# The weights of the second query convolution, made ready in the gate stage of an attention kernel

## The chip, the cores and the metric

The kernel runs on one core of a Trainium2 chip. The metric is the device time of one execution, in microseconds (us). An execution was also recorded by the hardware profiler. The engines are PE (TensorE, matrix multiplication), DVE (VectorE), ACT (ScalarE), POOL (GpSimd) and SP (SyncE, which here only issues DMAs). A line such as L1680 is a line of the kernel before.

## What is computed

Two layers, each an attention branch multiplied by a gated feed-forward branch and added to x. The edit concerns the first layer's second query convolution (`qc2_w`, 1024 x 1024 x 3 taps, causal, one group), and borders on the gate branch of the same layer:

```python
def _forward(x, w_qkv, w_o, qc1_w, qc1_b, qc2_w, qc2_b, kc1_w, ...):
    qkv = x @ w_qkv.T
    ...
    q = _causal_conv1d(_causal_conv1d(q, qc1_w, qc1_b, N_HEADS), qc2_w, qc2_b, 1)
    ...
    q = q.reshape(B, S, N_HEADS, HEAD_DIM) + 0.5 * k_mean[:, :, None, :]
    q = _rope(_l2norm(q.transpose(0, 2, 1, 3)), cos, sin)
    ...
def reference(...):                       # x is 2 x 1024 x 512
    xn = _layernorm(x)
    s = _L0_attn_ref(xn, ...)             # 16 query heads, 4 key heads of 64
    g = _silu(_L0_ffn_ref(xn, ...))       # relu(x up)^2 down, plus a routed part
    x = x + s * g
    ...                                   # second layer, untouched
```

## The kernel before

The program is a row of stages, one after another, that share on-chip buffers: the gate stage (names beginning a_, 13.5 to 320 us of the trace), the project stage (b_, q, k, v projections and the first convolutions, 320 to 589), the query stage (c_, the second query convolution, normalisation and rotation, 589 to 1051), attention (d_), then the second layer (e_, f_, h_). Each engine runs its own instruction list in program order, and semaphores are the only link between the lists. Nothing is scheduled at run time.

**Gate stage.** Four chunks of 512 tokens. For each, PE transposes the normalised tokens (`transposes`, L245), multiplies them with the latent and up weights (L273, 10 units of 12 matmuls, in chunk 0 in float32), then the logits and four output tiles (L300, L305). ACT copies the transposes out (`transposed`, L322 and L324), then one `relu` for each unit (L337), which must leave one of two PSUM banks before PE can fill it again. DVE squares each relu (L472), and after the units combines four output tiles. In the project stage `find_peaks` (L819) needs maxima that DVE takes over what ACT prepared at L890 to L892 from loaded weight rows.

**Query stage.** The three-tap convolution is done in a transformed form (six slices, fewer products than the taps would need). For each of 8 output tiles m of 128 channels, the float32 weight rows (128 x 3072) come in by DMA (L1256, L1476). DVE makes sums of taps (`sums`, L1673 and L1675), ACT scales and rounds a slice to fp16 (`highs`, L1457), DVE takes the rest to fp16 (`lows`, L1680). The scale needs the largest norm: ACT squares the rows (`ends_of`, L1469, L1472), PE adds them over partitions (`bound`, L1360), POOL takes a root, DVE inverts it (L1647 to L1656). PE then runs six slices of 24 matmuls (L1420). Around these stand DVE's `combine` (L1699 to L1727), which turns six slices into outputs, the squares and norms (L1498, L1330, L1336), the spreading of norms (L1353), DVE's `units` (L1750) and `remainder` (L1754), and POOL's rotation (L1599 to L1603). SP stores the finished parts (L1269, L1272) and loads the tables, the keys and `k_mean` (L1258) at the start.

## Time and profile before

| | |
|---|---|
| time, median of 3 (lowest to highest) | 2363.93 us (2362.97 to 2368.98) |
| profiled execution, its own time | 2369.5 us |
| its span | 2367.7 us |
| PE busy over the span | 2058.6 us, 87% |
| DVE, ACT, POOL busy | 1489.3, 1100.8, 771.9 us |
| gate stage | 13.5 to 320 us |
| project stage | 320 to 589 us |
| query stage | 589 to 1051 us |

Times in the trace are counted from the start of the span. "Busy" is the time with an instruction at work. In a timeline, what stands in brackets is how long the engine had been idle, and whose instruction released it. PEclk is the clock granted to PE, as a share of its full speed.

### The profile page before, as it was taken

The numbers are of one execution on the slowest core, as the hardware profiler recorded it, in microseconds if no ns is written. First come the engines' busy times: TensorE is split into PE (matmuls) and PEld (weight loads), VectorE is DVE, ScalarE is ACT, GpSimd is POOL, SyncE is SP. The second block draws the span as 40 slices with busy tenths as digits, with TensorE's granted clock in tenths as the row PEclk, the third lists the DMA queues.
The fourth block names the chain that finished last, engine by engine and source line by source line (L and its number), as shares of the span: only waits on it lengthen the run. The fifth ranks groups of instructions, "written<-read, shape, count | busy, mean of one in ns | idle before, by whom it ended". The sixth has DMA issues, their size and how long they took to land. (4 is left out here: it accounts for less than half of the span.)

```text
span 2367.7 us, 46673 instructions
## 1 busy us (share of the span) xinstructions
PE 2058.6 (87%) x19128; PEld 1009.8 (43%) x19128; DVE 1489.3 (63%) x2992; ACT 1100.8 (46%) x1987; POOL 771.9 (33%) x735
## 2 busy tenths in 40 slices
PE   7999989998647898979999789987588888888878
PEld 3444435555213333445555434443244444443434
DVE  3534354443559999716777725445888888888813
ACT  1212135555324333227777502324277777777760
POOL 0102212222447456504444402223343333433310
PEclk9999999999879899989999989997799999999999
DMA  6120101101412121362222264132936455364424
GB/s 240 36 89 36 67 19 32 32 14 44 140 43 83 54 67 32 107 208 75 90 82 76 76 175 143 58 79 76 216 59 84 69 72 81 58 89 65 59 79 142
DMA packets 149338, 198.03 MB, mean 84 GB/s; under 512 B 57154, under 2 KB 85956, under 8 KB 146564
## 3 DMA queue, kind: packets, MB, share of 16 engines
q1 hardware_dynamic: 147540, 181.41, 30.9%
q10 hardware_dynamic: 1584, 13.63, 1.6%
q8 instruction: 151, 2.47, 0.5%
q14 instruction: 63, 0.52, 0.1%
HBM read 134.69 MB, written 60.29 MB: 82 GB/s over the span
## 5 line engine op out<-in xcount | busy, mean ns | idle before, releaser
L3112 DVE TENSOR_REDUCE f_chunk_max<-f_ps_a 128x64 f32<-128x1024 f32 x320 | 319.7, 1033 | 47.4 <-PE f_ps_a L2856 25.0
L2985 ACT ACTIVATE conv_in<-f_ps_s 128x512 f32<-128x512 f32 x480 | 258.5, 602 | 86.6 <-PE f_ps_s L2887 42.7
L2856 PE MATMUL f_ps_a<-conv_in 128*32 128x512 bf16 (+3 forms) x3072 | 201.0, 340 | 42.1 <-DVE f_chunk_max L3112 25.4
L2078 ACT ACTIVATE d_probs<-d_ps_s,d_shift 128x512 f32<-128x512 f32 (+3 forms) x384 | 196.7, 584 | 82.7 <-PE d_ps_s L2017 72.8
L2887 PE MATMUL f_ps_s<-f_qs,f_ks 128*32 128x512 bf16 x2304 | 208.3, 382 | 23.3 <-ACT f_qs L2976 14.7
L1420 PE MATMUL c_ps_c<-conv_in,c_wT 128*128 128x512 f16 x768 | 186.2, 402 | 18.5 <-DVE c_odd L1721 14.1
L3052 POOL TENSOR_SCALAR f_absent<-f_rest 128x576 f32<-128x576 f32 x32 | 54.4, 1700 | 304.9 <-DVE f_rest L3129 180.7
L2909 PE MATMUL f_ps_o<-conv_in,f_v 128*32 128x512 f32 (+2 forms) x1152 | 125.9, 522 | 28.3 <-ACT conv_in L2985 27.4
L2976 ACT ACTIVATE f_qs<-f_ps_s 32x512 bf16<-32x512 f32 x192 | 112.8, 587 | 75.6 <-PE f_ps_s L2870 73.3
L2028 PE MATMUL d_ps_o<-d_probs,conv_in 128*64 128x512 f32 (+3 forms) x768 | 146.1, 488 | 0.0
L2856 PEld LDWEIGHTS f_ps_a<-conv_in 128*32 128x32 bf16 x3072 | 71.8, 98 | 164.3 <-DVE f_chunk_max L3112 68.6
L2388 PE MATMUL e_ps_s<-e_oT,conv_in 128*128 128x512 f32 x256 | 118.7, 626 | 23.2 <-DVEq L64 17.4
L2012 PE MATMUL d_ps_s<-conv_in 128*64 128x512 f16 (+3 forms) x768 | 126.4, 330 | 8.8 <-POOL d_ones L2086 8.8
L2145 DVE RECIPROCAL d_inverse<-d_ps_n 128x1024 f32<-128x1024 f32 x16 | 104.9, 6558 | 44.2 <-PE d_ps_n L2039 44.2
L1420 PEld LDWEIGHTS c_ps_c<-conv_in,c_wT 128*128 128x128 f16 x768 | 77.2, 103 | 129.9 <-issue 36.8
L2016 PE MATMUL d_ps_s<-conv_in 128*64 128x512 f16 (+3 forms) x384 | 124.8, 329 | 0.0
L2017 PE MATMUL d_ps_s<-conv_in 128*64 128x512 f16 (+3 forms) x384 | 124.7, 329 | 0.0
L300 PE MATMUL a_ps_d<-conv_in,conv_more 128*128 128x512 f32 x256 | 119.2, 621 | 0.0
L2887 PEld LDWEIGHTS f_ps_s<-f_qs,f_ks 128*32 128x32 bf16 x2304 | 59.6, 95 | 106.8 <-ACT conv_in L2985 35.0
L798 POOL TENSOR_TENSOR conv_in<-b_tiles,conv_in 128x1024 f16<-128x1024 f32 x16 | 34.1, 2131 | 186.6 <-ACT conv_more L958 186.6
L2388 PEld LDWEIGHTS e_ps_s<-e_oT,conv_in 128*128 128x128 f32 x256 | 51.0, 201 | 89.8 <-issue 82.4
L1420 PE MATMUL c_ps_c<-conv_more,c_wT 128*128 128x512 f16 x384 | 88.3, 384 | 0.0
(364 smaller groups left out, 4451.5 us busy)
## 6 DMA issues: line engine op xcount, KB each, us to landing
conv_in<-qk SPq DMA_DIRECT2D x96, 128.0 KB, 4.0
f_qs<-qk SPq DMA_DIRECT2D x96, 128.0 KB, 4.8
conv_in<-q_parts SPq DMA_DIRECT2D x8, 1024.0 KB, 5.1
o0T<-d_stage SPq DMA_DIRECT2D x16, 512.0 KB, 3.2
conv_in<-o0T SPq DMA_DIRECT2D x4, 2048.0 KB, 10.6
qk<-e_part SPq DMA_DIRECT2D x12, 640.0 KB, 4.9
f_qs<-qk SPq DMA_DIRECT2D x96, 64.0 KB, 4.7
rows<-in_qc_w ACTq DMA_DIRECT2D x3, 1536.0 KB, 7.0
```

What stands on the lines that cost most here:

```text
L1420: last = pe.matmul(ps_c[q % RING][:], wT[i][:, w, k, :], conv_of.of(t, x, k), start=(k == 0 and w == 0 and x == 0), stop=(k == MQ - 1 and ...
L2012: pe.matmul(out[sides[e], lo - low:], k_high[b][:, keys[e]], q[b][:, h, lo:hi], start=True, stop=False)
L2016: pe.matmul(out[sides[0], lo - low:], k_low[b][:, keys[0]], q[b][:, h, lo:hi], start=False, stop=True)
L2017: pe.matmul(out[sides[1], lo - low:], k_low[b][:, keys[1]], q[b][:, h, lo:hi], start=False, stop=True)\
L2028: last = pe.matmul(ps_o[a * HD0:(a + 1) * HD0, lo:hi], v[b][:, kt, :], probs[n % RING][a][:, lo:hi], start=(kt == 0), stop=((kt + 1) * P = ...
L2078: act.activation(probs[n % RING][SCORES[c][1]][:, lo:hi], ps_s[c % BANKS][:, lo - hi + CH:], ACT.Exp, bias=shift[:, 0:1], scale=HD0 ** -0. ...
L2388: last = pe.matmul(ps_s[t % 2][:], o_in[c % 2][:, m, t * P:(t + 1) * P], oT[:, m, :], start=(m == 0), stop=(m == MQ - 1))
L2856: last = pe.matmul(out[side(e), h, 0:w], qa[u][:, 2 * p + h, side(e, qt * P)], ka[u][:, kh * CH:kh * CH + w], start=True, stop=not last_keys)
L2887: last = pe.matmul(out[side(e), :], ks[u][:, side(e, kt * P)], qs[u][version][:, :, at:at + P], start=True, stop=not (masked or part))
L2909: last = pe.matmul(ps_o[2 * HD1 * h:2 * HD1 * (h + 1), lo - half * CH:], v[u][:, kt, :], probs[m % HELD][:, h, lo - half * CH:], start=(kt ...
L2985: act.activation(probs[m % HELD][:, :, at:at + P], bank_of["s", i, n][:].rearrange("p (h n) -> p h n", n=P), ACT.Exp, scale=HD1 ** -0.5).t ...
L3112: dve.tensor_reduce(chunk_max[:, qt - 2, :, at:at + w // CHUNK], src.rearrange("p h (c k) -> p h c k", k=CHUNK), AX.X, ALU.max).then_inc(a ...
```

## The change

All work on the weights of the second query convolution leaves the query stage and becomes 48 steps (8 tiles, 6 slices) in the gate stage. There, rows of two tiles are held in what will be the project stage's weight tile `b_wT`; sums lie in `b_xb0`, finished parts in `b_xb1` and `b_kc2T`, scratch in `b_c1T` and `b_kc1T`. The finished fp16 parts go to a DRAM tensor `conv_parts` in 512 KB stores, a ring of three. The project stage's loads (`weights.load`, `load_tokens`, `load_rows`) therefore stand behind the last of these stores. Two tables set where the steps go: `AFTER_UNIT` (after which unit of a chunk) and `BEFORE_TILE` (how many ahead of each output tile). On ACT a step's high part stands one relu later than the step's place among DVE's units. The scale comes from the row sums of absolute values: an ACT pass over 128 x 3072 with an accumulated sum, a DMA out and a broadcast back, a maximum on DVE. In the query stage the parts are loaded in halves of 1.5 MiB, 16 loads on SP; DVE, ACT, POOL and PE do no weight work there. The key of unit 1 is loaded ahead of the stores of unit 0.

```diff
@@ gate_phase: new parts
...
+        RING_W = 3
...
+        AFTER_UNIT = ((5, 6, 7), (1, 2, 4, 5, 7), (1, 2, 4, 5, 7), (1, 2, 4, 5, 7))
+        BEFORE_TILE = ((1, 1, 2, 3), (3, 2, 2, 2), (3, 2, 2, 2), (3, 2, 1, 0))
...
+        def w_source(s):
+            k, i = divmod(s, N_W)
+            return (w_sums[1], w_sums[0], w_sums[0], w_sums[1], w_rows[k % 2][:, 0], w_rows[k % 2][:, 2])[i]
+
+        def measure_w(act, k):
+            act.wait_ge(taken_in[k % 2], 16 * (k // 2 + 1))
+            if k > 0:
+                act.wait_ge(w_measured, k)
+            act.activation(w_spent, w_rows[k % 2].rearrange("p a n -> p (a n)"), ACT.Abs, accum_out=w_total[:, k:k + 1]).then_inc(w_measured, 1)
+            act.wait_ge(w_measured, k + 1)
+            act.dma_start(dram["conv_sizes"][k * P:(k + 1) * P].rearrange("(p n) -> p n", n=1), w_total[:, k:k + 1], allow_slow_non_contiguous=True)\
+               .then_inc(w_sent, 16)
+
+        def fetch_w(act, k):
+            act.wait_ge(w_sent, 16 * (k + 1))
+            if k >= 2:
+                act.wait_ge(w_sized_step, SIZE_STEPS * (k - 2) + 1)
+            act.dma_start(w_sized[k % 2], dram["conv_sizes"].rearrange("(a n) -> a n", a=1)[:, k * P:(k + 1) * P].to_broadcast((P, P)))\
+               .then_inc(w_fetched, 16)
+
+        def high_w(act, s):
+            if s >= W_ALL:
+                return
+            k, i = divmod(s, N_W)
+            act.wait_ge(w_sized_step, SIZE_STEPS * (k + 1))
+            if i < 4:
+                act.wait_ge(w_summed, N_W * k + (2, 3, 5, 6)[i])
+            if s >= RING_W:
+                act.wait_ge(w_stored[s % RING_W], 16 * (s // RING_W))
+            act.activation(w_made[s % RING_W][:, 0], w_source(s), ACT.Identity, scale=conv_scale[:, k % 2:k % 2 + 1]).then_inc(w_made_high, 1)
+            if i == 3 and k + 1 < MQ:
+                measure_w(act, k + 1)
+            if i == 4 and k + 1 < MQ:
+                fetch_w(act, k + 1)
+
+        def size_w(dve, k):
+            dve.wait_ge(w_fetched, 16 * (k + 1))
+            dve.tensor_reduce(w_size[:, 0:1], w_sized[k % 2], AX.X, ALU.max).then_inc(w_sized_step, 1)
+            dve.wait_ge(w_sized_step, SIZE_STEPS * k + 1)
+            dve.tensor_scalar(conv_unscale[:, k:k + 1], w_size[:, 0:1], 1e-30, SPREAD / FULL, ALU.max, ALU.mult).then_inc(w_sized_step, 1)
+            dve.wait_ge(w_sized_step, SIZE_STEPS * k + 2)
+            if k >= 2:
+                dve.wait_ge(w_made_low, N_W * (k - 1))
+            dve.reciprocal(conv_scale[:, k % 2:k % 2 + 1], conv_unscale[:, k:k + 1]).then_inc(w_sized_step, 1)
+
+        def sum_w(dve, k, i):
+            a0, a1, a2 = [w_rows[k % 2][:, a] for a in range(TAPS)]
+            s0, s1 = w_sums
+            to, first, by, second = ((s0, a2, 1.0, a0), (s1, a1, 1.0, s0), (s0, a1, -1.0, s0),
+                                     (s1, a2, 4.0, a0), (s0, a1, 2.0, s1), (s1, a1, -2.0, s1))[i]
+            if i == 0:
+                dve.wait_ge(taken_in[k % 2], 16 * (k // 2 + 1))
+            else:
+                dve.wait_ge(w_summed, N_W * k + i)
+            if i in (3, 4):
+                dve.wait_ge(w_made_low, N_W * k + i - 2)
+            elif i < 2 and k > 0:
+                dve.wait_ge(w_made_low, N_W * (k - 1) + 3 + i)
+            if by == 1.0:
+                dve.tensor_tensor(to, first, second, ALU.add).then_inc(w_summed, 1)
+            else:
+                dve.scalar_tensor_tensor(to, first, by, second, ALU.mult, ALU.add).then_inc(w_summed, 1)
+
+        def low_w(dve, s):
+            k = s // N_W
+            to = w_made[s % RING_W]
+            dve.wait_ge(w_made_high, s + 1)
+            dve.scalar_tensor_tensor(to[:, 1], w_source(s), conv_scale[:, k % 2:k % 2 + 1], to[:, 0], ALU.mult, ALU.subtract).then_inc(w_made_low, 1)
+
+        def weigh(dve, s):
+            k, i = divmod(s, N_W)
+            if k < MQ:
+                if i == 0:
+                    size_w(dve, k)
+                    sum_w(dve, k, 0)
+                    sum_w(dve, k, 1)
+                elif i < 4:
+                    sum_w(dve, k, (2, 3, 5)[i - 1])
+            if s > 0:
+                low_w(dve, s - 1)
+            if k < MQ and i == 2:
+                sum_w(dve, k, 4)
+
+        def take_in(sp, k):
+            sp.dma_start(w_rows[k % 2].rearrange("p a n -> p (a n)"), dram["qc2_w"][k]).then_inc(taken_in[k % 2], 16)
+
+        def store_w(sp, steps):
+            for s in [x - 1 for x in steps if x > 0]:
+                k, i = divmod(s, N_W)
+                sp.wait_ge(w_made_low, s + 1)
+                sp.dma_start(dram["conv_parts"][k, i // 3, :, i % 3], w_made[s % RING_W].rearrange("p a n -> p (a n)")).then_inc(w_stored[s % RING_W], 16)
+                if i == N_W - 1 and k + 2 < MQ:
+                    take_in(sp, k + 2)
...
@@ gate_phase: SyncE queue
-            for c in range(NCH - 1):
-                sp.wait_ge(xn_ready, c + 1)
-                sp.dma_start(x_in, x_rows[ds(c + 1, 1)].rearrange("a p t d -> p (a t) d")).then_inc(x_loaded, 16)
-                if c == 0:
-                    weights.load(sp)
-                store(c)
+            take_in(sp, 0)
+            take_in(sp, 1)
+
+            def load_x(c):
+                sp.wait_ge(xn_ready, c)
+                sp.dma_start(x_in, x_rows[ds(c, 1)].rearrange("a p t d -> p (a t) d")).then_inc(x_loaded, 16)
+
+            load_x(1)
+            store(0)
+            for c in range(NCH):
+                for u in AFTER_UNIT[c]:
+                    store_w(sp, at_unit(c, u))
+                if c + 2 < NCH:
+                    load_x(c + 2)
+                store_w(sp, at_tile(c, 0))
+                store_w(sp, at_tile(c, 1))
+                if c + 1 < NCH:
+                    store(c + 1)
+                store_w(sp, at_tile(c, 2))
+                store_w(sp, at_tile(c, 3))
+            for i in range(RING_W):
+                sp.wait_ge(w_stored[i], 16 * (W_ALL // RING_W))
+            weights.load(sp)
             sp.wait_ge(xnT_stored, 16 * 3)
             for h in range(2):
...
@@ gate_phase: ScalarE and VectorE
+                    if ML < u <= MI + ML:
+                        for s in at_unit(c, u - ML - 1):
+                            high_w(act, s)
+                    if c == 0 and u == ML + 3:
+                        measure_w(act, 0)
+                    if c == 0 and u == ML + 4:
+                        fetch_w(act, 0)
-            for c in range(NCH - 1):
-                transposed(c + 1)
-                products(c + 1)
-                silu(c)
+            for c in range(NCH):
+                for t in range(2):
+                    for s in at_tile(c, t):
+                        high_w(act, s)
+                if c + 1 < NCH:
+                    transposed(c + 1)
+                for t in range(2, TT):
+                    for s in at_tile(c, t):
+                        high_w(act, s)
+                if c + 1 < NCH:
+                    products(c + 1)
+                    silu(c)
+                    for s in at_unit(c, u):
+                        weigh(dve, s)
...
+                    for s in at_tile(c, t):
+                        weigh(dve, s)
...
@@ query_phase
+            def load_w(m, h):
+                if m >= 2:
+                    sp.wait_ge(slice_done, N_S * (m - 2) + 3 * (h + 1))
+                sp.dma_start(w_space[m % 2][h], dram["conv_parts"][m, h].rearrange("p i n -> p (i n)").bitcast(F32)).then_inc(w_loaded[m % 2][h], 16)
+
+            load_w(0, 1)
...
+            load_key(1)
+            load_w(2, 0)
+            store(0)
+            load_w(2, 1)
+            store(1)
+            for m in range(1, MQ):
+                if m == 1:
+                    store(B)
+                if m < MQ - 1:
+                    store(B * m + 1)
+                if m + 2 < MQ:
+                    load_w(m + 2, 0)
+                elif m == MQ - 1:
+                    sp.wait_ge(slice_done, N_S * m)
                     v_cols = dram["w_qkvT"].rearrange("p (k o) -> p k o", k=KD)[:, :, LAT + KVD:LAT + 2 * KVD]
                     sp.dma_start(v_w, v_cols).then_inc(v_loaded, 16)
                     load_v(0)
                     load_v(1)
-                store(g)
+                    store(B * m + 1)
+                store(B * m + 2)
+                if m + 2 < MQ:
+                    load_w(m + 2, 1)
...
-                    pe.wait_ge(w_ready, q + 1)
+                    if i % 3 == 0:
+                        pe.wait_ge(w_loaded[m % 2][i // 3], 16 * (m // 2 + 1))
...
-                highs(m, 5)
...
+            def coefs(m):
+                dve.wait_ge(coef_ready, 1)
+                dve.tensor_scalar(coef[m][:], wino_by[:], conv_unscale[:, m:m + 1], None, ALU.mult).then_inc(coef_ready, 1)
```

The removed functions are `highs`, `ends_of`, `load_rows`, `bound`, `root`, `size_of`, `scales`, `sums` and `lows` of the query stage, with their calls.

ACT in the gate stage, from the relus of chunk 2 to the transposes of chunk 3, before:

```order
L337 ACTIVATE a_relu<-a_ps_m,a_w_unscale 128x512 x8
L339 ACTIVATE a_logits<-a_ps_m 128x32
L351 ACTIVATE rows<-conv_more 128x512 x4
L355 DMA g<-rows 128x2048
L322 ACTIVATE a_xnT<-a_ps_t 128x512
L324 ACTIVATE a_x_parts<-a_ps_t 128x512
```

The same place after, from the last logits of chunk 2 on (L469 and L471 the copies of the transposes, L252 is a high part, L505 the gate's rows, L231 the sum of absolute values, L233 and L240 its way out and back):

```order
L252 ACTIVATE b_xb<-b_wT,a_conv_scale 128x1024
L240 DMA b_kc1T<-conv_sizes 128x128
L505 ACTIVATE rows<-conv_more 128x512 x4
L509 DMA g<-rows 128x2048
L252 ACTIVATE b_kc2T<-b_wT,a_conv_scale 128x1024
L252 ACTIVATE b_xb<-b_xb,a_conv_scale 128x1024 x2
L252 ACTIVATE b_kc2T<-b_xb,a_conv_scale 128x1024
L252 ACTIVATE b_xb<-b_xb,a_conv_scale 128x1024
L231 ACTIVATE b_c1T,a_w_total<-b_wT 128x3072
L233 DMA conv_sizes<-a_w_total 128x1
L469 ACTIVATE a_xnT<-a_ps_t 128x512
L471 ACTIVATE a_x_parts<-a_ps_t 128x512
```

Between those logits and the first copy of the transposes there are now six high parts and one pass over 128 x 3072.

SP, the loads of the project stage (`b_...` from inputs), which before stood early in the gate stage:

```order
L220 DMA conv_in<-in_x 128x2048
L552 DMA b_wT<-in_w_qkvT 128x6144
L553 DMA b_c1T<-in_qc_wT 128x1536
L554 DMA b_kc1T<-in_kc_wT 128x384
L555 DMA b_kc2T<-in_kc_wT 128x1536
L557 DMA b_bias<-in_qc_b 128x8x1
L557 DMA b_bias<-in_kc_b 128x2x1 x2
L561 DMA b_bias_crossed<-in_qc_b 64x8x1 x2
L561 DMA b_bias_crossed<-in_kc_b 64x2x1 x2
L216 DMA xnT<-a_xnT 128x4x512
```

After, they stand at its end, behind the last stores of the parts (L313):

```order
L313 DMA conv_parts<-b_xb 128x2048 x2
L313 DMA conv_parts<-b_kc2T 128x2048
L718 DMA b_wT<-in_w_qkvT 128x6144
L719 DMA b_c1T<-in_qc_wT 128x1536
L720 DMA b_kc1T<-in_kc_wT 128x384
L721 DMA b_kc2T<-in_kc_wT 128x1536
L723 DMA b_bias<-in_qc_b 128x8x1
L723 DMA b_bias<-in_kc_b 128x2x1 x2
L727 DMA b_bias_crossed<-in_qc_b 64x8x1 x2
L727 DMA b_bias_crossed<-in_kc_b 64x2x1 x2
L738 DMA b_xb<-xnT 128x4x256 x4
L732 DMA conv_in<-in_w_qkv 128x8x512
```

The eleven loads moved past all of the gate stage's other work, the seven short bias loads (L723, L727) among them.

DVE in one tile of the query stage, from the norms (L1738) to a shuffle (L1734), before:

```order
L1738 TENSOR_SCALAR c_norm<-c_ps_n 128x32
L1652 TENSOR_SCALAR c_w_scale<-c_size 128x1
L1654 RECIPROCAL c_size<-c_w_scale 128x1
L1656 TENSOR_SCALAR c_coef<-c_wino,c_size,unscale 128x6
L1675 SCALAR_TENSOR_TENSOR c_sums<-rows,c_sums 128x1024
L1699 SCALAR_TENSOR_TENSOR c_even<-c_ps_c,c_coef,c_odd 128x512
L1701 SCALAR_TENSOR_TENSOR c_odd<-c_ps_c,c_coef,c_odd 128x512
L1680 SCALAR_TENSOR_TENSOR c_wT<-c_sums,c_w_scale,c_wT 128x1024
L1675 SCALAR_TENSOR_TENSOR c_sums<-rows 128x1024
L1680 SCALAR_TENSOR_TENSOR c_wT<-c_sums,c_w_scale,c_wT 128x1024
L1675 SCALAR_TENSOR_TENSOR c_sums<-rows,c_sums 128x1024
L1734 STREAM_SHUFFLE c_swapped<-c_raw 128x1024
```

The same place after (L1784 is the norm, L1745 to L1752 the combining, L1780 the shuffle, L1796 the units):

```order
L1784 TENSOR_SCALAR c_norm<-c_ps_n 128x32
L1745 SCALAR_TENSOR_TENSOR c_even<-c_ps_c,c_coef,c_odd 128x512
L1747 SCALAR_TENSOR_TENSOR c_odd<-c_ps_c,c_coef,c_odd 128x512
L1780 STREAM_SHUFFLE c_swapped<-c_raw 128x1024
L1750 SCALAR_TENSOR_TENSOR c_ps_c<-c_ps_c,c_coef,c_square 128x512
L1752 SCALAR_TENSOR_TENSOR c_ps_c<-c_ps_c,c_coef,c_square 128x512
L1796 TENSOR_TENSOR c_turned<-c_turned,c_ps_b 128x512 x2
```

Sums, low parts and scales are gone from between the combining steps; what is left keeps its order.

## Rows read from the trace of the kernel before

**Rows 1.** Busy time by stretch of the program: start:end, length, then the columns named.

```profile
core 0: us, PE busy (x) PEld busy (x) DVE busy (x) ACT busy (x) POOL busy (x), PEclk, DMA share, GB/s
13.50:320.00 306.50, 291.91 (x965) 140.98 (x966) 121.11 (x219) 60.91 (x103) 50.30 (x40) 0.96 0.22 80
...
737.60:956.40 218.80, 191.60 (x851) 82.25 (x851) 211.04 (x202) 80.99 (x112) 121.94 (x45) 0.92 0.18 53
956.40:992.30 35.90, 35.58 (x169) 15.45 (x167) 24.51 (x30) 7.79 (x11) 21.60 (x8) 1.00 0.42 117
```

**Rows 2.** Timeline of PE, query stage: start, length, form, [idle before <-releaser].

```profile
607.91 1.48 PE L1330 MATMUL c_ps_n<-c_square,c_head_sum 128*32 128x512 f32 x4 [2.45 <-ACT c_square L1498]
...
658.06 2.34 PE L1330 MATMUL c_ps_n<-c_square,c_head_sum 128*32 128x512 f32 x4 [16.35 <-ACT c_square L1498]
...
682.23 8.07 PE L1420 MATMUL c_ps_c<-conv_in,c_wT 128*128 128x512 f16 x24 [14.12 <-DVE c_odd L1721]
...
737.65 7.93 PE L1420 MATMUL c_ps_c<-conv_in,c_wT 128*128 128x512 f16 x36
...
814.32 2.15 PE L1353 MATMUL c_ps_b<-c_strip_t,c_head_spread 32*128 32x512 f32 x4 [5.33 <-ACT c_strip_t L1508]
...
816.40 7.55 PE L1420 MATMUL c_ps_c<-conv_in,c_wT 128*128 128x512 f16 x24
```

**Rows 3.** Groups by line, query stage: busy, mean ns, idle before.

```profile
L1680 DVE SCALAR_TENSOR_TENSOR c_wT<-c_sums,c_w_scale,c_wT 128x1024 f16<-128x1024 f32 x32 | 49.7, 1552 | 11.1 <-ACT c_wT L1457 10.8
...
L1675 DVE SCALAR_TENSOR_TENSOR c_sums<-c_rows,c_sums 128x1024 f32<-128x1024 f32 x12 | 30.2, 2513 | 0.3
...
L1457 ACT ACTIVATE c_wT<-c_sums,c_w_scale 128x1024 f16<-128x1024 f32 x32 | 36.7, 1147 | 74.9 <-DVE c_coef L1656 31.7 <-DVE c_sums L1675 30.2 <-issue 12.7
```

**Rows 4.** Timelines of DVE and POOL, 925 to 938 us.

```profile
926.58 3.38 DVE L1673 TENSOR_TENSOR c_sums<-c_rows 128x1024 f32<-128x1024 f32 x1
...
929.99 1.23 DVE L1673 TENSOR_TENSOR c_sums<-c_rows,c_sums 128x1024 f32<-128x1024 f32 x1
...
936.92 1.29 DVE L1680 SCALAR_TENSOR_TENSOR c_wT<-c_sums,c_w_scale,c_wT 128x1024 f16<-128x1024 f32 x1
...
925.65 3.23 POOL L1603 TENSOR_TENSOR c_turned<-c_turned,c_swapped 128x1024 f32<-128x1024 f32 x1
```

**Rows 5.** Timelines of PE, ACT and DVE, gate stage.

```profile
176.31 26.06 PE L273 MATMUL a_ps_m<-a_x_parts,conv_in 128*128 128x512 f16 x120
...
225.34 0.60 ACT L322 ACTIVATE a_xnT<-a_ps_t 128x512 f32<-128x512 f32 x1 [17.19 <-PE a_ps_t L245]
...
297.01 0.55 DVE L461 TENSOR_SCALAR conv_more<-conv_more,a_mv,a_rstd 128x512 f32<-128x512 f32 x1 [0.67 <-POOL a_rstd L393]
```

**Rows 6.** Groups by line, gate stage.

```profile
L472 DVE TENSOR_TENSOR conv_more<-a_relu 128x512 f32<-128x512 f32 x32 | 26.6, 831 | 67.5 <-ACT a_relu L337 67.5
```

**Rows 7.** Timeline of ACT at the start of the project stage.

```profile
319.75 0.52 ACT L890 ACTIVATE conv_in<-conv_in 128x384 f32<-128x384 f32 x1 [2.92 <-PEq L75]
...
320.27 1.04 ACT L892 ACTIVATE conv_in<-conv_in 128x1024 f32<-128x1024 f32 x1
```

**Rows 8.** SP's queue (timeline), and DMA issues with microseconds to landing.

```profile
16.38 16.00 SPq L557 DMA_DIRECT2D b_bias<-in_kc_b  x2
...
593.71 5.62 SPq L1258 DMA_DIRECT2D c_k_mean<-k_mean  x1
...
b_wT<-in_w_qkvT SPq DMA_DIRECT2D x1, 3072.0 KB, 17.6
...
conv_in<-in_w_qkv SPq DMA_DIRECT2D x1, 2048.0 KB, 12.2
...
rows<-in_qc_w ACTq DMA_DIRECT2D x3, 1536.0 KB, 7.0
```

**Rows 9.** Timelines of DVE and PE after the start of the project stage.

```profile
327.89 0.17 DVE L984 TENSOR_REDUCE b_most<-b_sums 128x2 f32<-128x16 f32 x1
...
333.35 0.38 PE L819 MATMUL b_ps_w<-ident,b_most 128*3 128x128 f32 x2
```

More of the change, by code:

```diff
@@ L70, in wait_apart, with gate_phase @@
     engine.sem_inc(ticks, 1)
-def gate_phase(nc, sem, dram, ident, half, weights, space):
+def gate_phase(nc, sem, dram, ident, half, weights, space, conv_unscale):
     with ExitStack() as ctx:
@@ L1136, in query_phase @@
         strips = sb("strips", [P, BLK, NCH, STRIP])
-        total = [sb(f"total{i}", [P, 1]) for i in range(2)]
         RING, SPREADS = 4, 2
@@ L1300, in _ @@
             load_v(3)
+            store(LAST - 2)
             sp.wait_ge(slice_done, N_S * MQ)
@@ L1353, in spread @@
                 pe.matmul(ps_b[c % SPREADS][:], head_spread[strip, :], strip_t[strip, :], start=True, stop=True).then_inc(spread_done, 1)
-            def bound(k):
-                pe.wait_ge(ends_summed, ENDS * (k + 1))
-                if k > 0:
-                    pe.wait_ge(w_step, W_STEPS * (k - 1) + 1)
-                pe.matmul(ps_x[:, 0:1], ones[:], total[k % 2][:], start=True, stop=True).then_inc(bound_done, 1)
             def norms(j, step):
@@ L1400, in hook @@
                         norms(j, step)
-                if m == 0 and h == 5:
-                    bound(1)
-                if m + 2 < MQ and h == BOUND_AT:
-                    bound(m + 2)
             def emptied(m, i):
```

270 lines of the change are left out of this document (69 added, 201 removed).

## The prediction

> **What bounds the kernel now.** I read the windows first. In the gate stage PE is busy 291.9 of 306.5 us and is granted 0.96 of its clock, while DVE is busy 121.1 and ACT 60.9 [rows 1]. PE sets the end there, and the other two have room on paper. In the query stage it is the reverse. Over tiles 2 to 6 (737.6 to 956.4) DVE is busy 211.0 of 218.8 us, PE 191.6 at a clock of 0.92. Tile 7 has no weights left to make for a next tile, and it takes 35.9 us with DVE busy only 24.5 and PE 35.6 at full clock [rows 1]. So tiles 2 to 6 take 43.8 us on average because of DVE, and 35.9 would be PE's own pace. The timeline of PE then shows where the start of the stage loses: 16.35 us of waiting at 658.06 and 14.12 at 682.23, both for what DVE and ACT get round to late [rows 2]. The groups by line give the prices of the weight work: a low part costs 1.55 us on average, a sum up to 2.51, a high part on ACT 1.15 [rows 3]. The timelines beside POOL show why the means are high: a sum takes 3.38 us while POOL runs and 1.23 when it doesn't, a low part 1.29 [rows 4].
>
> **What is removed, and what that gives.** The tiles are counted from PE's first slice group to the next tile's.
> - Tiles 2 to 7: six at tile 7's pace give 6 x 35.9 = 215.4 us. Before, they took 992.3 − 737.65 = 254.6 [rows 1, 2]. Gain 39.2; I keep 38, since the loads are new to SP's queue.
> - Tile 1 took 737.65 − 682.23 = 55.4 us [rows 2]; the key's work lies in it too, which stays. I take 51, a gain of 4.4, a little over half of the 7.9 by which a later tile shrinks (43.8 to 35.9).
> - Tile 0, with what is ahead of it: 682.23 − 607.91 = 74.3 us. The wait of 16.35 is for a square on ACT [rows 2], which stands behind high parts and sums of tile 1. I let it shrink by 12.7, and 5 more go with the lows between the slices: 17.7.
> - Against it, 3 MiB more of weights are issued ahead of the tables and `k_mean`. A load of 1.5 MiB landed 7.0 us after its issue, the issue of `k_mean` took 5.62 us of SP's queue [rows 8]. Two such loads one after the other are 14, side by side 7. I take 9.5.
>
> Query stage: 9.5 − 17.7 − 4.4 − 38 = **−50.6 us**, bounds −42 (tiles at 37, tables 14 late, partly offset by tile 1) and −56 (tables 7 late, tile 1 at 47).
>
> **What is added to the gate stage.** A tile of weights costs DVE six sums at 1.23, six lows at 1.29 [rows 4] and some 0.7 for the scale, which no row shows: 15.8 us, for 8 tiles 126. With the 121.1 of before that is 247 of 306.5 us [rows 1]. It costs ACT six highs at 1.04 and the pass over 128 x 3072. That one has no row; from 0.52 us for 384 and 1.04 for 1024 elements [rows 7] it is 2.7 (same slope) to 3.1 (in proportion). I take 3.0. Eight times (6.2 + 3.0) is 74 us, on top of 60.9. Neither engine is full, so throughput alone hides it all. What doesn't hide is the order. PE has two banks in the units, 2.6 us each (26.06 for ten [rows 5]), so a relu that is over 2.6 us late stops PE. DVE's squares wait 67.5 us in total for the relus [rows 6], which is where the steps after the units lie. I walked the lists by hand, chunk by chunk:
> - chunk 0: the measuring pass ahead of a relu, +1.6;
> - transposes of chunk 2: +4.8. ACT has highs and a pass of 3.0 ahead of the first copy. It was idle 17.19 us there [rows 5], but each high waits for DVE's sum, and DVE for the output tile;
> - units of chunk 2: +1.0 and +1.6 where a high and a relu meet, and +3.4 where the measuring pass sits in front of relu 7: 6.0;
> - transposes of chunk 3: +7.7. In the order above six highs and the pass, 9.4 us of work, stand ahead of the copies, and the highs come at DVE's pace;
> - units of chunk 3: +5.
>
> That is 25.1 on PE, and 23.6 for the last low part, since the tail of the last output tiles has slack of 1.5. I add 7 for the clock: after a wait of 5.33 us 24 matmuls took 7.55 us, where 36 took 7.93 elsewhere, so 5.3 for 24 [rows 2]. The list above has three waits of that size or near it, at about 2.3 us each. Gate stage: **+31 us**, bounds +15 (highs and lows run without waiting on each other) and +45 (ten of the steps in PE's way wait for a POOL instruction, whose mean there is 50.3/40 = 1.3 us [rows 1], +13).
>
> The row says a two-input DVE instruction takes 3.38 us beside POOL's 3.23 and 1.23 without [rows 4]. The Trainium skill, page "SBUF — State Buffer", section "SBUF: two separate sides", says DVE and GpSimd share a port pair under an exclusive lock that is held for a whole instruction. The row agrees with it. By that rule every step that meets POOL pays, as in my upper bound, and the gate stage would come to some +44; by the walk, where most steps meet no POOL instruction, it is +31.
>
> **The transition.** The project stage's loads must wait for the last store. In the time of before, the last low would be done with the last normalising, at 297.0 + 0.55 [rows 5] and one more low, 298.9; its store lands some 3.3 later, at 302.2. Then 9.4 MiB are loaded: weights 4.7, tokens 2, rows 2.75. On SP's queue two bias loads took 16.00 us by themselves [rows 8]; with the four large issues (2 us), the other bias loads (4) and the tokens (2.5) the row loads are issued about 24.5 us on, and the 2 MiB landed 12.2 us after the issue [rows 8]: 36 to 37. I take 36, bounds 28 (the bias loads cost half) and 42 (transfers queue; 3 MiB by itself landed 17.6 us after its issue [rows 8]). ACT then starts the maxima at 302.2 + 36 = 338.2, where it started at 319.75 [rows 7], 18.5 later. PE has about 5 us of slack there (DVE's maximum is ready at 328.06, PE takes it up at 333.35 [rows 9]). So **+13.5 us** beyond the gate stage's delay, bounds +5 and +22.
>
> The load of two short bias vectors keeps SP's queue 16.00 us [rows 8]. The page "DMA: Bandwidth & Descriptors" of the Trainium skill, section "Rules for kernel authors", says that a strided last dimension becomes one descriptor for each element; that speaks against moving these loads to a place where others wait behind them, and no run here shows yet what they cost there.
>
> **The sum.** 31 + 13.5 − 50.6 = −6.1 us on the profiled execution of 2369.5, so 2363.4. That execution lies 5.6 above the median of the runs (2363.93). Taken off, **2358 us**. The rest of the program is untouched. A difference of 0.3%, 7 us, is about what a measurement of this kernel can tell from none.
>
> **Rivals.**
> - *The gate stage saturates* (0.22, slower). Sum, high and low of a step are a chain over two engines, 1.23 + 1.04 + 1.29, 3.6 us, and a ring of three parts must be stored before it is reused. If each of 48 steps leaves DVE waiting 1.04 for its high, 50 us of DVE's 59 free ones are gone (306.5 − 247), and if about half of it, 27, reaches PE: 31 + 27 = 58, and 58 + 13.5 − 50.6 = +21, **2385 us**. For it: DVE's waits in the units are short, 67.5 over 32 squares is 2.1 us each [rows 6], less than a sum and a low together. Against it: in each step the low is of the step before, so the high has time. It decides for slower once the gate stage loses over 44.
> - *The gate stage hides most* (0.20, faster): +15, transition 13.5 or less (say 13), −50.6: −22.6, **2341 us**. For it: DVE free for 59 us, ACT's 17.19 of idle time ahead of each chunk's copies [rows 5]. Against it: PE is busy 95% of the stage, so nothing that stops it is regained.
> - *The query tiles don't reach 35.9* (0.08): the units, remainder and key work of POOL and DVE hold each at 39, as POOL is busy 121.9 of 218.8 and each remainder beside it takes longer [rows 1, 4]. 6 x 3.1 = 18.6 of the gain go: **2376 us**.
> - The forecast's own case (0.50): 35 to 55 lost in gate stage and transition, 45 to 55 regained, so 2344 to 2374.
>
> **Chances.** The forecast's case lies near the bound of 7 us: of its 0.50 I count 0.23 as faster, 0.25 as the same, 0.02 as slower. The rival with a hidden gate stage is faster (0.19 of 0.20), the saturated one slower (0.20 of 0.22), the slow tiles slower (0.06 of 0.08). Faster 0.42, same 0.30, slower 0.28. Range 2332 to 2383: below it lie only a gate stage at its lower bound with a query stage at its upper one, above it the worse half of the saturated case.
>
> **What would show it.** Right: windows of the gate stage with DVE busy near 245 us and PE's share down to about 0.87; the last `conv_parts` store near 330; ACT's first maximum of the project stage near 369; tiles of the query stage at 36 us, PE at full clock. Wrong: waits of PE in the gate stage on relus or copies that total over 45 us or under 12; rows that land within 25 us of the last store; PE in the query stage still waiting for DVE between slices; a first slice that waits for its half tile of weights.

## The result, and the profile after

The changed kernel takes 2383.11 us (median of 4, 2381.49 to 2386.41) against 2363.68 before; the ratio is 1.0079 (95% interval 1.006 to 1.0098). It is slower by 19 us, where 2358 us, slightly faster than before, was forecast; the forecast's range ended at 2383. The profiled execution has a span of 2384.6 us, 16.9 more than before.

The windows: first the gate stage before, up to the end of PE's last output tile (13.5 to 310.6); then after, the same stretch (13.5 to 370.3) and tiles 2 to 7 of the query stage:

```profile
core 0: us, PE busy (x) PEld busy (x) DVE busy (x) ACT busy (x) POOL busy (x), PEclk, DMA share, GB/s
13.50:310.60 297.10, 291.58 (x964) 140.81 (x964) 116.71 (x211) 60.03 (x101) 49.74 (x39) 0.97 0.22 79
```

```profile
13.50:370.30 356.80, 301.05 (x964) 145.50 (x964) 242.90 (x331) 134.68 (x165) 57.58 (x39) 0.90 0.45 154
...
799.10:1012.20 213.10, 212.40 (x1010) 93.19 (x1008) 108.74 (x154) 40.45 (x60) 124.32 (x48) 1.00 0.36 112
```

DVE's busy time in the gate stage rose by what was reckoned: it is 242.9 us, 126 more than before. PE has the same 964 matmuls, at a clock of 0.90 in place of 0.97, and the stage is 59.7 us longer. Tiles 2 to 7 take 213.1 us at full clock, with DVE busy for half of it.

PE's timelines: first its last output tile of the gate stage before (302.04); then, after, its largest waits in the gate stage, the same last output tile (361.59), `find_peaks`, and the marks of the query stage:

```profile
302.04 7.03 PE L300 MATMUL a_ps_d<-conv_in,conv_more 128*128 128x512 f32 x16
```

```profile
97.07 2.09 PE L392 MATMUL a_ps_t<-ident,conv_more 128*128 128x128 f32 x8 [8.75 <-ACT a_x_parts L471]
...
185.17 2.09 PE L392 MATMUL a_ps_t<-ident,conv_more 128*128 128x128 f32 x8 [18.33 <-ACT a_x_parts L471]
...
272.96 2.10 PE L392 MATMUL a_ps_t<-ident,conv_more 128*128 128x128 f32 x8 [10.68 <-ACT a_x_parts L471]
...
361.59 7.03 PE L447 MATMUL a_ps_d<-conv_in,conv_more 128*128 128x512 f32 x16
...
404.95 0.59 PE L985 MATMUL b_ps_w<-ident,b_most 128*3 128x128 f32 x2 [4.73 <-DVE b_most L1151]
...
687.21 2.35 PE L1498 MATMUL c_ps_n<-c_square,c_head_sum 128*32 128x512 f32 x4 [15.58 <-ACT c_square L1622]
...
726.63 2.34 PE L1498 MATMUL c_ps_n<-c_square,c_head_sum 128*32 128x512 f32 x4 [7.40 <-ACT c_square L1622]
...
749.90 7.56 PE L1577 MATMUL c_ps_c<-conv_in,c_w_early 128*128 128x512 f16 x24 [15.61 <-DVE c_odd L1767]
...
799.10 7.94 PE L1577 MATMUL c_ps_c<-conv_in,rows 128*128 128x512 f16 x36
```

The first three wait for ACT's copies of the transposes. `find_peaks` starts at 404.95, where it started at 333.35 [rows 9]. Square, first slice and tile 2 at 687.21, 749.90 and 799.10 answer to 607.91, 682.23 and 737.65 [rows 2]. From these marks, and from PE's last output tile of the gate stage (start 302.04 before, 361.59 after):

| piece | forecast | measured | how |
|---|---|---|---|
| gate stage | +31 | +59.5 | 361.59 − 302.04 |
| transition | +13.5 | +12.1 | (404.95 − 333.35) − 59.5 |
| up to the first square | +9.5 | +7.7 | 282.3 against 274.6 after `find_peaks` |
| tile 0 | −17.7 | −11.6 | 62.7 against 74.3 |
| tile 1 | −4.4 | −6.2 | 49.2 against 55.4 |
| tiles 2 to 7 | −38 | −41.6 | 213.1 against 254.7 |
| the rest | 0 | −3.0 | 1372.4 against 1375.4 |
| sum | −6.1 | +16.9 | |

All but one of the terms lie within about 6 us. The gate stage is 28.5 us off. (Two traces of the same gate stage differ too: in kernel 10 below, which has it unchanged, the last output tile starts at 359.78. So a difference of 2 us between such marks tells nothing.)

What holds the stage up is seen on ACT and DVE around 163 us, in the changed kernel's timelines:

```profile
163.33 0.19 ACT L231 ACTIVATION_READ_ACCUMULATOR b_c1T<-b_wT 128x1 f32 x1
...
163.54 0.33 ACTq L233 DMA_DIRECT2D conv_sizes<-a_w_total  x1
...
173.40 0.33 ACTq L240 DMA_DIRECT2D b_kc1T<-conv_sizes  x1
...
173.83 1.15 ACT L252 ACTIVATE b_kc2T<-b_wT,a_conv_scale 128x1024 f16<-128x1024 f32 x1 [8.71 <-DMA conv_sizes<-a_w_total]
...
167.85 0.69 DVE L666 BATCH_NORM_STATS2 a_stats<-conv_more 128x6 f32<-128x512 f32 x1
...
177.24 0.28 DVE L260 TENSOR_REDUCE a_w_size<-b_kc1T 128x1 f32<-128x128 f32 x1 [8.69 <-DMA b_kc1T<-conv_sizes]
```

ACT has the row sums at 163.5 and issues their way out to DRAM. One high part later it stands for 8.71 us until they have landed, and only then issues the broadcast back (173.40). DVE, which has the output tile to do next, first needs the scale, and stands 8.69 us until 177.24. From the end of the sum (163.52) to DVE's maximum it is 13.7 us. The same trace's DMA issues, with KB and us to landing:

```profile
conv_sizes<-a_w_total ACTq DMA_DIRECT2D x8, 0.5 KB, 8.1
...
b_kc1T<-conv_sizes ACTq DMA_DIRECT2D x8, 64.0 KB, 5.3
...
c_k_mean<-k_mean SPq DMA_DIRECT2D x1, 1024.0 KB, 18.0
```

The waits for the way out add up to 45.4 us on ACT (18.5, 13.3, 7.6 and 6.0 before four different instructions), those for the way back to 17.1 on DVE.

### The profile page after: what moved, and what is told of

Its sections match the earlier page's. It is cut to its first block and busy times, and to the rows that moved or that the text cites. A ratio compares the mean times of both kernels' runs of the same rounds, so it can differ in the third digit from the quotient of the medians.

```text
span 2384.6 us, 46640 instructions
## 1 busy us (share of the span) xinstructions
PE 2049.2 (86%) x19112; PEld 1009.6 (42%) x19112; DVE 1432.5 (60%) x2993; ACT 1092.6 (46%) x1939; POOL 747.7 (31%) x726
## 5 line engine op out<-in xcount | busy, mean ns | idle before, releaser
L2387 PE MATMUL e_ps_s<-e_oT,conv_in 128*128 128x512 f32 x256 | 112.6, 600 | 22.5 <-DVEq L65 16.7
L3072 POOL TENSOR_TENSOR f_diag<-ident,f_missed 128x1536 bf16<-128x1536 f32 x32 | 88.1, 2753 | 0.0
L1577 PE MATMUL c_ps_c<-conv_more,c_w_late 128*128 128x512 f16 x384 | 86.9, 379 | 0.0
L420 PE MATMUL a_ps_m<-a_x_parts,conv_in 128*128 128x512 f16 x360 | 80.7, 385 | 6.1 <-ACT a_relu L484 4.9
```

Of the source, the lines that this page charges most:

```text
L2387: last = pe.matmul(ps_s[t % 2][:], o_in[c % 2][:, m, t * P:(t + 1) * P], oT[:, m, :], start=(m == 0), stop=(m == MQ - 1))
```

## The experiments

Ratios are to the runs of the kernel before on the same chip. To compare kernels measured on different chips, each ratio is multiplied by 2363.7 us; the changed kernel is then 18.7 us above the kernel before, written +18.7. "Less" and "more" below are differences of these figures.

**1. Without the round trip.** `measure_w` keeps its pass, the DMAs go, and each partition takes its scale from its own sum; the maximum over partitions is left out:

```diff
-            dve.wait_ge(w_fetched, 16 * (k + 1))
-            dve.tensor_reduce(w_size[:, 0:1], w_sized[k % 2], AX.X, ALU.max)
+            dve.wait_ge(w_measured, k + 1)
+            dve.tensor_reduce(w_size[:, 0:1], w_total[:, k:k + 1], AX.X, ALU.max)
```

> Leaves out the maximum over partitions: each partition takes its scale from its own row sum, so the way of the sums out to DRAM and back (a DMA out, a broadcast in, eight times) is gone; the pass over 128 x 3072, the sums, highs, lows and their order stay. Theory A (the round trip): the trace of the changed kernel shows ACT standing 45.4 us in all for the sums' DMA and DVE 17.1 us for the one back, and of the 59 us by which the gate stage grew some 25 to 30 go with it: about 2356 us. Rival B (sheer work and order on ACT and DVE fill the stage): the waits only move to the next step, gain under 8 us: 2376 to 2383 us.

2350.29 us, ratio 0.9934 (0.991 to 0.9958), which is −15.6: 34 us less than the changed kernel, and faster than before. PE in its trace:

```profile
162.89 2.09 PE L385 MATMUL a_ps_t<-ident,conv_more 128*128 128x128 f32 x8 [9.10 <-ACT a_x_parts L464]
...
246.06 2.09 PE L385 MATMUL a_ps_t<-ident,conv_more 128*128 128x128 f32 x8 [7.15 <-ACT a_x_parts L464]
...
327.75 7.03 PE L440 MATMUL a_ps_d<-conv_in,conv_more 128*128 128x512 f32 x16
...
371.21 0.59 PE L978 MATMUL b_ps_w<-ident,b_most 128*3 128x128 f32 x2 [6.63 <-DVE b_most L1144]
```

The wait of 8.75 at the first copies is gone, the others are 9.10 and 7.15, the last output tile comes 33.8 us earlier (327.75 for 361.59) and `find_peaks` 33.7. Theory A holds, by more than expected. Against the kernel before, the gate stage is still 25.7 us longer.

**2. Without the pass over 128 x 3072 as well.**

```diff
         def measure_w(act, k):
+            return
...
-            dve.wait_ge(w_fetched, 16 * (k + 1))
-            dve.tensor_reduce(w_size[:, 0:1], w_sized[k % 2], AX.X, ALU.max).then_inc(w_sized_step, 1)
+            dve.wait_ge(taken_in[k % 2], 16 * (k // 2 + 1))
+            dve.tensor_reduce(w_size[:, 0:1], w_rows[k % 2][:, 0, 0:P], AX.X, ALU.max).then_inc(w_sized_step, 1)
```

The scale comes from 128 values of the rows, so this kernel leaves the bound out; it is read for its time alone.

> As the kernel without the round trip, and the pass over 128 x 3072 is left out too (the scale comes from 128 values of the rows, which is not a bound). Theory A: ACT loses 8 x 2.94 us of work, of which 3 to 8 us reach PE, since the passes stand before relus and copies: about 2350 us. Rival B: ACT's work is what fills the stage, and 15 us or more of the 23.5 come off: 2360 us or less against 2380 without the trip alone.

2342.66 us, 0.9902 (0.9875 to 0.993), 7.6 us less than without the trip alone; every one of its times (2338.5 to 2343.6) lies below every one of kernel 1 (2347.64 to 2355.54). By the medians, a third of ACT's 23.5 us reaches PE. The two traces show more: PE's last output tile starts at 314.10 here, 13.7 us earlier than in kernel 1, but the one is the fastest execution of its kernel and the other the slowest. Rival B would have had 15 or more; it is less by the medians, and not by much by the traces.

**3. The bias loads early.**

```diff
             load_x(1)
+            weights.load_biases(sp)
             store(0)
```

> The seven short bias loads stand early in the gate stage again, all else as changed. Theory A: SP's queue spent 15.8 us on them (363.60 to 379.44) ahead of the token and row loads, the rows then landed 12.7 to 13.8 us after their issue; ACT's first maximum comes 10 to 13 us earlier, time 2371 us. Rival C: the transition is bound by the bytes of the large loads, under 3 us gained: 2381 us.

2376.86 us, 1.0058 (1.0041 to 1.0075), 5 us less, and the interval overlaps that of the changed kernel (1.006 to 1.0098). SP's queue first after the change and ACT's first maximum, then the same with the biases early:

```profile
358.32 0.32 SPq L313 DMA_DIRECT2D conv_parts<-b_kc2T  x1
...
363.60 11.75 SPq L723 DMA_DIRECT2D b_bias<-in_kc_b  x2
...
381.78 0.89 SPq L732 DMA_DIRECT2D conv_in<-in_w_qkv  x1
...
396.51 0.52 ACT L1056 ACTIVATE conv_in<-conv_in 128x384 f32<-128x384 f32 x1 [20.14 <-DMA conv_in<-in_qc_w]
```

```profile
358.34 13.38 SPq L742 DMA_DIRECT2D b_xb<-xnT  x4
...
371.77 2.12 SPq L736 DMA_DIRECT2D conv_in<-in_w_qkv  x1
...
389.38 0.52 ACT L1060 ACTIVATE conv_in<-conv_in 128x384 f32<-128x384 f32 x1 [18.60 <-DMA conv_in<-in_qc_w]
```

With the biases gone the queue stands at the next load in line, the tokens, for 13.38 us, where the biases had 11.75. The rows are issued 10 us earlier, but the last store is 4.7 us earlier too, by other differences of the gate stage, and ACT gains 7.1 in all: 2.4 in the transition. Theory A, which had 10 to 13, fails: the queue stands in the same place whichever load is next. The 2.4 is what rival C has; that the bytes are what binds is not shown by it. The biases stand in their new place as well: 13.10 us from 15.37 on, behind the first weight rows and tokens. So the form of the bias loads may still play a part; no run has them with no large load ahead.

**4. Copies of the transposes first.**

```diff
-                for t in range(2):
-                    for s in at_tile(c, t):
-                        high_w(act, s)
                 if c + 1 < NCH:
                     transposed(c + 1)
-                for t in range(2, TT):
+                for t in range(TT):
```

> ACT copies the transposes of the next chunk before the highs of the first two output tiles. Theory A: PE's waits of 8.75, 18.33 and 10.68 us between the two halves of the transposes go, but the trip then holds back DVE's output tiles and PE's third tile, so 5 to 15 us gained: 2373 us. Rival B (the order on ACT is what costs, not the trip): nearly all of the 36 us come back: 2350 us.

2403.6 us, 1.0167 (1.0139 to 1.0195): 21 us more. Both theories are wrong on the sign.

```profile
128.23 22.52 PE L420 MATMUL a_ps_m<-a_x_parts,conv_in 128*128 128x512 f16 x96 [16.79 <-ACT a_latent L478]
...
184.18 9.81 PE L447 MATMUL a_ps_d<-conv_in,conv_more 128*128 128x512 f32 x16 [9.37 <-DVE conv_more L661]
...
283.14 9.82 PE L447 MATMUL a_ps_d<-conv_in,conv_more 128*128 128x512 f32 x16 [7.36 <-DVE conv_more L661]
```

The waits at the copies are gone, and in their place PE waits for latents (16.79) and output tiles (9.37, 7.36). By the order of the lists, the highs come after the copies, DVE needs the highs in front of the output tiles, and the next chunk's latents stand behind all of it.

**5. The sizes added on PE**, a full version of the first: a matrix of ones in the lent `b_kc1T`, one matmul for each tile of weights at a place in PE's list where ACT's pass should be done, and DVE reads PSUM.

```diff
+        def add_sizes(pe, k):
+            pe.wait_ge(w_ones_set, 1)
+            pe.wait_ge(w_measured, k + 1)
+            pe.matmul(size_in(k)[:, 0:1], w_sized[0], w_total[:, k:k + 1], start=True, stop=True).then_inc(w_fetched, 1)
```

> A full version of the kernel without the round trip: PE adds the row sums over partitions with a matrix of ones (one matmul of 128 x 1 each for the 8 tiles, put where ACT's pass should be done), DVE reads PSUM; the scale comes from the total, not the largest, row sum. Theory A (the round trip is what the gate stage lost): the time of the kernel that leaves the maximum out, 2350 us, within 3 us. Rival B: PE now waits for ACT's passes itself, and 5 us or more of the gain are lost again: 2355 us or more.

2348.26 us, 0.9932 (0.9909 to 0.9954). All of the gain is there with a scale that is a bound for all partitions (their total in place of the largest). PE waits for a sum ahead of two of the eight (0.59 and 1.24 us), which the time doesn't show. Theory A holds.

**6. Steps later, by the table alone.**

```diff
-        BEFORE_TILE = ((1, 1, 2, 3), (3, 2, 2, 2), (3, 2, 2, 2), (3, 2, 1, 0))
+        BEFORE_TILE = ((1, 1, 2, 3), (1, 2, 3, 3), (1, 2, 3, 3), (3, 2, 1, 0))
```

> Only the table of steps ahead of the output tiles is changed, in chunks 1 and 2 from 3, 2, 2, 2 to 1, 2, 3, 3, so that three highs and not five stand ahead of the copies of the transposes, and the scale of tile 3 is needed only after them. Theory D (what matters is how much of the chain lies ahead of the copies): PE's waits of 18.33 and 10.68 us there shrink by 15 or more together, of which 8 to 12 stay gained: 2373 us. Rival E (as with the copies put first, the waits only move to the output tiles and the next latents): within 4 us of 2383.

2378.65 us, 1.0062 (1.0046 to 1.0078), 4 us less, and not told apart from the changed kernel by the intervals.

```profile
171.61 2.09 PE L392 MATMUL a_ps_t<-ident,conv_more 128*128 128x128 f32 x8 [5.92 <-ACT a_x_parts L471]
...
203.84 22.77 PE L420 MATMUL a_ps_m<-a_x_parts,conv_in 128*128 128x512 f16 x96 [6.11 <-ACT a_latent L478]
...
287.21 15.97 PE L420 MATMUL a_ps_m<-a_x_parts,conv_in 128*128 128x512 f16 x60 [8.81 <-ACT a_latent L478]
```

Of the waits of 18.33 and 10.68 at the copies 5.92 is left, but 6.11 and 8.81 stand at the latents, where there were none above 1.2. So of the 23 us that left the copies some 15 show up at the latents. The time is at the edge of what rival E allows, and short of theory D.

**7. Loads early.** Rows, half of the large weight tile, and `b_c1T` in chunk 3, biases at the start.

```diff
                 store_w(sp, at_tile(c, 1))
+                if c == NCH - 1:
+                    sp.wait_ge(m_done, before(NCH))
+                    weights.load_rows(sp)
+                    sp.wait_ge(w_made_low, N_W * (MQ - 1))
+                    sp.wait_ge(w_measured, MQ)
+                    weights.load_first(sp)
```

> Of the project stage's loads the biases go back to the start, and the rows (2.75 MiB), half of the large weight tile and the first convolution's weights are issued in chunk 3 as soon as their buffers are free, ahead of the last six stores; 4 MiB instead of 9.4 stay behind the last store. Theory F (the transition is bound by bytes and by a queue that stands after a few large loads, whatever load comes next: with the biases moved the token loads took 13.38 us of SP's queue instead): ACT's first maximum no longer waits for rows, PE's start 10 us or more earlier: 2368 us or less. Rival G (the early loads hold back the last stores and with them the last steps): 2375 us or more.

2374.97 us, 1.0043 (1.0027 to 1.0058), 8.5 us less.

```profile
380.76 12.49 PE L1024 MATMUL b_ps<-b_xb,b_wT 128*128 128x512 f32 x24 [14.43 <-DMA b_xb<-xnT]
...
393.18 0.38 PE L999 MATMUL b_ps_w<-ident,b_most 128*3 128x128 f32 x2
```

`find_peaks` is 11.8 us earlier and no longer waits, but the stage's first matmuls start only 6 us earlier (380.76 for 386.82). They wait for the tokens, which stand behind the last store. The time lies between theory F (2368 or less) and rival G (2375 or more).

**8. The three together (5, 6 and 7).**

> The three of these together: sizes added on PE, late steps, early loads. If the parts add up: 2383 - 32 - 10 - 15 = 2326 us. If they take from the same wait (without the trip there is less left for the table to gain): 2335 us.

2330.19 us, 0.9851 (0.9824 to 0.9878), −35.2. Two of the sizes are added at other places of PE's list than in kernel 5. The parts add up to −47 from the changed kernel, and −54 are measured, a difference that the intervals of the four kernels don't tell from none. Nothing here speaks against the parts simply adding up. The later steps seem to give the same with the trip and without it: PE's last output tile is 7.0 us earlier in kernel 6 than in the changed kernel (354.63), and 7.5 earlier here than in kernel 5 (317.19 for 324.74). PE has three waits above 2 us left in the gate stage; the largest, and the one for a size:

```profile
194.61 4.45 PE L438 MATMUL a_ps_m<-a_x_parts,conv_in 128*128 128x512 f16 x12 [3.68 <-ACT a_relu L511]
...
244.95 0.35 PE L263 MATMUL a_ps_m<-a_w_total,b_kc1T 128*128 128x1 f32 x2 [2.44 <-ACT b_c1T L237]
```

**9. The way back issued by SP.**

```diff
-            if i == 4 and k + 1 < MQ:
-                fetch_w(act, k + 1)
...
                 if i == N_W - 1 and k + 2 < MQ:
                     take_in(sp, k + 2)
+                if i == 3 and k + 1 < MQ:
+                    fetch_w(sp, k + 1)
```

> The round trip stays as it is, but its way back is issued by SP (behind the store of the slice after which ACT measures), so that ACT no longer stands waiting for the way out to land. Theory A1 (the loss is ACT standing 45.4 us with highs, copies and relus behind it): 15 to 22 of the 33 us that the trip costs are gained, 2366 us. Theory A2 (the loss is the trip's length, out and back, for which DVE and with it the chain of steps must wait whoever issues it): under 8 us gained, 2376 us or more.

2381.59 us, 1.0069 (1.0042 to 1.0095), 2.4 us less, no difference that can be told. DVE's group that waits for the way back, then PE, then SP's last store:

```profile
L258 DVE TENSOR_REDUCE a_w_size<-b_kc1T 128x1 f32<-128x128 f32 x8 | 2.3, 282 | 29.6 <-DMA b_kc1T<-conv_sizes 29.6
...
180.76 2.09 PE L393 MATMUL a_ps_t<-ident,conv_more 128*128 128x128 f32 x8 [12.79 <-ACT a_x_parts L472]
...
270.05 2.10 PE L393 MATMUL a_ps_t<-ident,conv_more 128*128 128x128 f32 x8 [12.72 <-ACT a_x_parts L472]
...
352.83 7.03 PE L448 MATMUL a_ps_d<-conv_in,conv_more 128*128 128x512 f32 x16
...
354.74 0.32 SPq L311 DMA_DIRECT2D conv_parts<-b_kc2T  x1
```

ACT no longer stands for the sums' DMA, and DVE stands 29.6 us instead of 17.1; ACT's largest group of highs now waits 80.9 us for DVE, where it was 55.3. PE does gain in the gate stage: its last output tile is 8.8 us earlier (352.83 for 361.59). But the last store is only 3.6 us earlier (354.74 for 358.32) and `find_peaks` 3.3 (401.62 for 404.95), since the project stage's loads stand behind that store. So ACT's standing cost PE something on the way, and next to nothing at the end. By these marks the end is set by the last step of the chain, and for it the length of the trip counts, whoever issues the way back: theory A2.

**10. Tables and `k_mean` ahead of the half tiles.**

```diff
-            load_w(0, 1)
...
-            load_w(1, 0)
-            load_w(1, 1)
...
             sp.dma_start(k_mean[:], dram["k_mean"]).then_inc(tables, 16)
+            load_w(0, 1)
+            load_w(1, 0)
+            load_w(1, 1)
```

> In the query stage the three half tiles of weights that were issued ahead of the tables and k_mean are issued behind them; all else as changed. The first norms wait for k_mean (16.37 us on DVE, 15.58 on PE), which landed 18.0 us after its issue. Theory H (4.5 MiB ahead in the queue set this): 6 to 9 us gained, 2375 us. Rival I (the queue stands for its own loads anyhow, and the weights' lateness then stops tile 0's second half): under 3 us, 2381 us.

2373.79 us, 1.0039 (1.0021 to 1.0056), 9.5 us less. SP's load of `k_mean` in the changed kernel, then here, then PE here:

```profile
668.39 11.52 SPq L1413 DMA_DIRECT2D c_k_mean<-k_mean  x1
```

```profile
665.39 2.02 SPq L1410 DMA_DIRECT2D c_k_mean<-k_mean  x1
...
675.19 2.35 PE L1498 MATMUL c_ps_n<-c_square,c_head_sum 128*32 128x512 f32 x4 [5.19 <-ACT c_square L1622]
...
737.84 7.55 PE L1577 MATMUL c_ps_c<-conv_in,c_w_early 128*128 128x512 f16 x24 [15.61 <-DVE c_odd L1767]
```

The same load takes 11.52 us of the queue behind the three half tiles and 2.02 ahead of them. PE's wait of 15.58 is 5.19; the one before tile 1 (15.61) is what it was, and it names DVE's combining, not a load. Theory H holds.

**11. All four.**

> Sizes on PE, late steps, early loads and tables first together. Theory H: 6 us less than the three together, 2324 us. Rival I: 2330 us, as the three.

2318.94 us, 0.9809 (0.9781 to 0.9836), 45 us less than before, and 10 less than the three together (theory H had 6). Its gate stage up to 330 us, with columns as above:

```profile
13.50:330.00 316.50, 294.95 (x980) 141.26 (x980) 248.47 (x339) 133.91 (x165) 59.12 (x40) 0.96 0.49 183
```

DVE has 248 us of work in 316 there, and PE's clock is 0.96, close to what it was before.

**12. The kernel before, with `k_mean` ahead of the weight rows.**

```diff
-            sp.dma_start(rows[1].rearrange("p a i o -> p (a i o)"), dram["qc2_w"][1]).then_inc(rows_loaded[1], 16)
...
             sp.dma_start(k_mean[:], dram["k_mean"]).then_inc(tables, 16)
+            sp.dma_start(rows[1].rearrange("p a i o -> p (a i o)"), dram["qc2_w"][1]).then_inc(rows_loaded[1], 16)
```

> The kernel before with one edit: the load of weight rows that stood ahead of k_mean (1.5 MiB) is issued behind it. It shows how much of what the tables' place gives has nothing to do with the change. Theory H: the first norms wait there too (9.46 us on ACT), so 2 to 4 us are gained, 2361 us. Rival: DVE is the limit of that stage and takes the gain back, within 1 us of before.

2360.12 us, 0.9977 (0.9962 to 0.9992), 5 us less. In its trace ACT waits 5.04 us for `k_mean` ahead of the first squares, where it was 9.46. So a part of what the tables' place gives, about half by the medians, was there without the change; this kernel moves 1.5 MiB, kernel 10 moves 4.5.

## Why the prediction was wrong

**The step that failed** is in "What is added to the gate stage": "some 0.7 for the scale, which no row shows". That counted the three small instructions on DVE (0.6 us by the trace) and put the way of the sums at nothing. The change sends 128 numbers to DRAM and back, 8.1 and 5.3 us to landing, 13.7 us from the sum to DVE's maximum, in a chain of steps whose next sum, high and low can't start without it. Without it the kernel takes 2350.3 or, in the full version, 2348.3 us: the trip costs 34 us, where the forecast had none. Small loads of the kernel before would have given the price, such as that of the key's temperature (0.5 KB, 7.7 us to landing), but the round trip had no line in my sum, and no row was read for it.

The miss is 25 us, not 34, because the rest was forecast too high by some 9. Without the trip the gate stage is 25.7 us longer than before, where +31 was forecast, and there are small differences in the other pieces. These errors happened to point the other way. That the time came out at the end of the range is luck as well: that end was set by the saturated gate stage, which is not what happened.

**The walk** of the lists was otherwise near in its sum: with the trip taken out `find_peaks` comes at 371.21, +37.9 on before, where 31 + 13.5 = 44.5 was forecast. The transposes of chunk 2 and 3 were put at 4.8 and 7.7; without the trip PE waits 9.10 and 7.15 there. With the trip it was 18.33 and 10.68, and 8.75 in chunk 1, where nothing was forecast. The prices were near: 126 us of busy time added on DVE, 2.75 + 0.19 for the pass, and sums and lows as in the changed kernel's groups (busy, mean ns). A high was priced at 1.04 though [rows 3] has 1.15, and 1.15 is what it took:

```profile
L231 ACT ACTIVATE b_c1T<-b_wT 128x3072 bf16<-128x3072 f32 x8 | 22.0, 2748 | 0.0
...
L260 DVE TENSOR_REDUCE a_w_size<-b_kc1T 128x1 f32<-128x128 f32 x8 | 2.2, 279 | 17.1 <-DMA b_kc1T<-conv_sizes 17.1
...
L284 DVE SCALAR_TENSOR_TENSOR b_xb<-b_wT,b_xb 128x1024 f32<-128x1024 f32 x24 | 30.2, 1258 | 1.1
...
L290 DVE SCALAR_TENSOR_TENSOR b_xb<-b_xb,a_conv_scale 128x1024 f16<-128x1024 f32 x24 | 32.7, 1361 | 0.1
...
L290 DVE SCALAR_TENSOR_TENSOR b_xb<-b_wT,a_conv_scale,b_xb 128x1024 f16<-128x1024 f32 x8 | 12.2, 1531 | 3.1 <-ACT b_xb L252 3.1
```

**The clock** was put at 7 us. PE's busy time in the gate stage rose by 9.5 us (291.6 to 301.1 for the same matmuls). In kernel 1, without the trip's waits, it is 295.6, a rise of 4.1; so the trip's 34 us hold some 5 of clock.

**The rule on the port**, that DVE and GpSimd share a port pair which one of them holds for a whole instruction (the Trainium skill, "SBUF — State Buffer", "SBUF: two separate sides"), would have put the gate stage at some +44 by waits on POOL. The trace shows little of it: DVE's 96 sums and lows average 1.26 to 1.53 us, by group, against 1.23 and 1.29 undisturbed [rows 4], and together take 128 us instead of 121. These waits come to 7 us of DVE's time at most, and are not what made the stage long.

**The transition** was right in size (12.1 for 13.5; from the first load's issue at 361.02 to ACT's first maximum it is 35.5 us, for 36) and partly for a wrong reason: the 16 us that were put on the bias loads move to the next load when the biases are gone (kernel 3).

**The query stage** gave 51.7 us for 50.6, and 3 more came behind it. That it fits to 1 us is luck: tile 0 gave 6.1 less, and the other three pieces made up for it. Tiles 2 to 7 take 35.5 each, PE's pace. In tile 0 the wait of 16.35 [rows 2] shrank to 7.40, by 9 and not by the forecast 12.7, and the one at its end did not shrink but went from 14.12 to 15.61. `k_mean` has no part in that: kernel 10 has it early, and its tile 0 takes 62.7 us as well (675.19 to 737.84). (The bound of −56 for this stage adds up to −57 from its own terms, which changes nothing.)

**The rivals.** The saturated gate stage gave the right time (58 and 2385 us) by the wrong mechanism. It had DVE wait 1.04 us for each high, 50 us in all; in the changed kernel's groups all 48 lows together wait 3 us. The runs also show a stage with the same work that is 34 us shorter without the trip, and one (kernel 11) in which 248 us of DVE's work fit in 316. What remains open is how the remaining 26 us of the gate stage in kernel 1 divide between the measuring passes (7.6 by the medians, up to 13.7 by the traces) and the order of the steps.

**The signs.** DVE is busy 242.9 us, for the forecast 245, and the query tiles run at PE's pace. PE's share of the gate stage is 0.84 for 0.87, the last store is issued at 358 for 330, and ACT's first maximum comes at 396.5 for 369. PE's waits on relus and copies come to 49 us, which the prediction had named, from 45 on, as a sign that it is wrong.
